# A feed-forward block on one core: the second stage as two nested levels of seven products

## What is computed

```python
def _L0_cond_ref(x, weight, bias, lora_a_weights, lora_b_weights, scaling_factors, adapter_id):
    base = jnp.einsum('bsi,oi->bso', x, weight) + bias
    a_sel = lora_a_weights[adapter_id]
    b_sel = lora_b_weights[adapter_id]
    scale = scaling_factors[adapter_id]
    low = jnp.einsum('bsi,bri->bsr', x, a_sel)
    delta = jnp.einsum('bsr,bor->bso', low, b_sel)
    return base + scale[:, None, None] * delta

def _L0_ffn_ref(x, codes, absmax, bias):
    w = _dequant_nf4(codes, absmax)
    out = jnp.einsum('bsd,od->bso', x, w)
    return out + bias

x = x + _L0_ffn_ref(_L0_cond_ref(x, ...), codes, absmax, bias)
```

## Time and profile before

| what | value |
|---|---|
| median of 3 runs | 2213.1 us (2212.15 to 2213.67) |
| span of the profiled execution | 2211.8 us, 1.3 us under the median of the runs |
| TensorE busy | 2166.8 us (98%) |
| VectorE busy | 1790.3 us (81%) |
| ScalarE busy | 1016.5 us (46%) |
| GpSimd busy | 46.8 us (2%) |
| DMA | 558.00 MB, mean 252 GB/s |
| granted TensorE clock | 0.994 of full |

### The profile page before, as it was taken

One profiled execution on the slowest core, in us unless ns is written; L12 is line 12 of the kernel. 1 busy time (PEld: TensorE's weight loads), 2 busy tenths in 40 slices (PEclk: granted clock), 3 DMA queues, 4 the chain that ended last, 5 costly groups with the idle time before them and its releaser, 6 DMA issues.

```text
span 2211.8 us, 31548 instructions
## 1 busy us (share of the span) xinstructions
PE 2166.8 (98%) x12104; PEld 1859.8 (84%) x12104; DVE 1790.3 (81%) x2647; ACT 1016.5 (46%) x1277; POOL 46.8 (2%) x55
## 2 busy tenths in 40 slices
PE   4899999999999999999999999999999999999999
PEld 4688788788878778899999988888988889888888
DVE  8899889768974664688778898888898887988887
ACT  8655555555553333444444443343443434443432
POOL 5100000000000000000000000000000000000000
PEclk8999999999999999999999999999999999999999
DMA  9688788887887897777777887777977877877775
GB/s 285 218 255 268 226 260 267 261 257 240 271 260 237 276 306 228 270 239 239 234 244 233 271 283 240 241 245 246 304 251 240 253 245 257 289 249 246 239 244 173
DMA packets 381172, 558.00 MB, mean 252 GB/s; under 512 B 23376, under 2 KB 234992, under 8 KB 380896
## 3 DMA queue, kind: packets, MB, share of 16 engines
q1 hardware_dynamic: 377712, 544.95, 77.6%
q0 software_dynamic: 3312, 11.03, 1.6%
HBM read 427.96 MB, written 128.99 MB: 252 GB/s over the span
## 4 chain that ended last, share of the span: by engine, by line
PE 91%; DVE 4%; DMA 3%; issue 1%; ACT 0%; SPq 0%; DVEq 0%; ACTq 0%
PE ps L1441 26%; PE ps L1273 14%; PE ps L1275 14%; PE ps L1274 14%; PE ps L1442 13%; PE ps L1445 4%; PE ps L1288 2%; PE ps L1444 2%; DMA rq<-xc_d 1%; PE ps L1321 1%; PE ps L1269 1%; DMA xc_d<-rq 1%; DMA xr<-xc_d 0%; DVE low_tw L966 0%; DVE tile L987 0%
## 5 line engine op out<-in xcount | busy, mean ns | idle before, releaser
L1441 PE MATMUL ps<-comb,xs 128*128 128x512 f32 x2527 | 903.3, 395 | 0.8 <-DVE comb L1047 0.8
L767 ACT CAST xs<-xr 128x1024 fp32r<-128x1024 f32 x427 | 448.3, 1051 | 629.8 <-DMA xr<-xc_d 628.9
L1442 PE MATMUL ps<-comb,xs 128*128 128x256 f32 x2527 | 707.8, 280 | 0.0
L1053 DVE TENSOR_TENSOR xs<-xr,xs 128x1024 fp32r<-128x1024 f32 x427 | 521.4, 1221 | 130.8 <-ACT xs L767 127.8
L1441 PEld LDWEIGHTS ps<-comb,xs 128*128 128x128 f32 x2527 | 474.3, 188 | 103.5 <-DVE comb L1047 1.1
L1442 PEld LDWEIGHTS ps<-comb,xs 128*128 128x128 f32 x2527 | 475.4, 188 | 14.5
L1273 PE MATMUL ps<-wq,tile 128*128 128x512 f32 x1088 | 468.2, 430 | 1.9 <-DVE tile L987 1.8
L1275 PE MATMUL ps<-wq,tile 128*128 128x512 f32 x1088 | 427.5, 393 | 0.0
L1274 PE MATMUL ps<-wq,tile 128*128 128x512 f32 x1088 | 426.1, 392 | 0.0
L1273 PEld LDWEIGHTS ps<-wq,tile 128*128 128x128 f32 x1088 | 205.2, 189 | 70.1 <-ACT cs L735 3.5
L1275 PEld LDWEIGHTS ps<-wq,tile 128*128 128x128 f32 x1088 | 204.9, 188 | 45.0
(11 more groups left out here) (119 smaller groups left out, 2219.8 us busy)
## 6 DMA issues: line engine op xcount, KB each, us to landing
xr<-xc_d SPq DMA_DIRECT2D x427, 512.0 KB, 4.0
raw<-in_L_cond_weight_dram SPq DMA_DIRECT2D x128, 512.0 KB, 4.8
xc_d<-rq SPq DMA_DIRECT2D x26, 1792.0 KB, 7.5
res<-in_x_dram SPq DMA_DIRECT2D x64, 512.0 KB, 5.2
out_dram<-res SPq DMA_DIRECT2D x128, 256.0 KB, 4.5
wc_d<-cs SPq DMA_DIRECT2D x32, 896.0 KB, 4.6
comb_raw<-wc_d SPq DMA_DIRECT2D x28, 1024.0 KB, 7.8
x_nat<-in_x_dram SPq DMA_DIRECT2D x104, 256.0 KB, 3.9
```

The source lines that it names most:

```text
L767: nc.scalar.copy(xs[f][:, HI, :, :], xr[f][:, LO, :, :]).then_inc(s_xhi, 1)
L1053: tt(xs[f][:, LO, :, :], xr[f][:, LO, :, :], xs[f][:, HI, :, :].bitcast(F32), ALU.subtract).then_inc(s_xlo, 1)
L1441: nc.tensor.matmul(bank[:, :], x_hi, both, start=(k == 0), stop=False)
L1442: nc.tensor.matmul(bank[:, 0:HW], x_lo, high, start=False, stop=False)
```

## The change

Stage 2 becomes two nested levels of seven products. The outer level is the seven combinations that stage 1 still makes (now with a 2 x 2 split of the full output, columns in halves of 1024 and inner dimension in halves of 1024); the inner level splits each outer product once more. The loop is over 56 units u = 8i + q: i is the outer combination (order `OUTER`), q the batch entry, and in each unit seven inner products k (order `INNER`) for two row tiles at once: 7 x 4 blocks x 3 matmuls with 512 output columns.

- **Inner weight sums**: SP loads four blocks of `wc_d` into `tb`, GpSimd makes four sums of 1024 elements (`sum_blocks`), SP stores them to `wi_d` and loads them from there as weights, in halves. This is done twice for each outer product.
- **Inner x sums**: SP loads two 512 KB blocks into `xg` once a unit, VectorE makes four sums of 512 elements (`sum_x`), then ScalarE and VectorE split seven tiles of 512 elements (`x_hi`, `x_lo`).
- **Adding up**: products 0, 2, 4, 6 accumulate in one PSUM bank or pair of banks, 1 and 3 in another; VectorE reads the running value after each product and adds it to `r_sb` (in the first and last eight units ScalarE copies four of the seven). TensorE waits for the reading of product k before it starts product k + 2 (`evacuated`). The sums of outer products go to `m_d` in DRAM and come back as a base (`load_base`, `load_total`); output rows are stored from unit 32 on.
- In units 0 to 31 the 512 columns are cut in two matmuls of 256, the second with 16 columns of lora A in four products of seven. From unit 32 on they are one matmul of 512.
- The residual is an identity matrix added to the combined weight in stage 1 (16 matmuls of 128 columns).
- In the last eight units (u from 48 on) two totals are finished: GpSimd and VectorE each add 2048 elements (`add_last`).
- The jobs of the last strip of stage 1 also load blocks, make inner sums and split the first weights.

Core of the diff (stage 2 of each engine; loads of the last strip of stage 1, lora and constants left out):

```diff
 # SP
+            for u in range(NU):
+                i, q = divmod(u, QB)
+                turn = q == QB - 1 and i < LAST
+                if 1 <= u <= BOTH:
+                    store_sums(u - 1, 1)
+                if u > BOTH:
+                    for m in range(2):
+                        store_total(u - 1, m)
+                if u + 1 < NU:
+                    sp.wait_ge(s_xlo, NF * (u + 1))
+                    load_x(u + 1)
+                if u + 1 < LOWS:
+                    load_a(u + 1)
...
+                for k in range(NF):
+                    if turn:
+                        sp.wait_ge(s_prod, NF * u + k + 1)
+                        for c in range(2):
+                            load_half_comb(i + 1, INNER[k], c)
+                    if k == 1 and QB <= u + 1 < BOTH:
+                        load_base(u + 1)
...
+                    if k == 1 and u >= BOTH:
+                        for m in range(2):
+                            load_total(u, m)
+                    if k == 3 and i < LAST:
+                        if q == 1:
...
+                            load_blocks(i + 1, 0)
+                        if q == 3:
+                            for n in range(4):
+                                store_sum(i + 1, 0, n)
+                            load_blocks(i + 1, 1)
+                        if q == 5:
+                            for n in range(4):
+                                store_sum(i + 1, 1, n)
+                if u < BOTH:
+                    store_sums(u, 0)
 # GpSimd
+            def sum_blocks(i, c):
...
+                tt(b11, b12, b11, ALU.subtract).then_inc(s_ws, 1)
+                pool.wait_ge(s_wl[B22], arrived[B22])
+                tt(b12, b22, b12, ALU.subtract).then_inc(s_ws, 1)
+                pool.wait_ge(s_ws, 4 * n + 1)
+                tt(b22, b22, b11, ALU.subtract).then_inc(s_ws, 1)
...
+                tt(b21, b21, b22, ALU.subtract).then_inc(s_ws, 1)
+            def add_last(u):
...
+                pool.wait_ge(s_lev, 4 * (u - BOTH + 1))
+                tt(total[1][:, :, :, :], total[1][:, :, :, :], r_sb[u % 2][:, :, :, :], ALU.add).then_inc(s_fin[1], 1)
+            for u in range(NU):
+                i, q = divmod(u, QB)
+                if i < LAST and q in (2, 4):
+                    sum_blocks(i + 1, q // 2 - 1)
+                if u >= BOTH:
+                    add_last(u)
 # VectorE
+    LO_STEPS = {2: [0], 3: [1], 4: [2, 3], 5: [4], 6: [5, 6], 7: [7], 8: [8, 9], 9: [10], 10: [11, 12], 11: [13]}
+            for u in range(NU):
+                i, q = divmod(u, QB)
+                for k in range(NF):
...
+                    if not fresh(u) or k not in COPIED:
+                        add_product(u, k)
...
+                    if u >= BOTH and k == 5:
+                        add_lora_pair(u, 0)
+                        add_lora_pair(u, 1)
+                    if u >= BOTH and k == 6:
+                        add_last(u)
+                        add_lora_pair(u, 2)
+                        add_lora_pair(u, 3)
...
+                    if k == 1 and u + 1 < LOWS:
+                        a_difference(u + 1)
...
+                    if u + 1 < NU and k in (2, 3, 4):
+                        sum_x(u + 1, {2: (0, 1), 3: (2,), 4: (3,)}[k])
+                    if u + 1 < NU:
+                        for f in {3: (A11, SS1), 4: (S2,), 5: (S4, S3), 6: (A12, A22)}.get(k, ()):
+                            x_lo(u + 1, f)
+                    for n, h in lo_halves(u, k):
+                        comb_lo(n, h)
 # TensorE
+            def multiply(u, k):
...
+                if k in (2, 3, 4, 6):
+                    evacuated(u, {2: 0, 3: 1, 4: 2, 6: 4}[k])
...
+                for kt in range(QT):
...
+                    if not split:
+                        ins = three(big[:, bank, :], x_hi, x_lo, w_hi[:, 0:SW], w_lo[:, 0:SW], first, last and not lora,
+                                    not opens)
+                        continue
+                    for n, (x, w) in enumerate(((x_hi, w_hi), (x_hi, w_lo), (x_lo, w_hi))):
+                        begin, end = first and n == 0, last and n == 2
+                        nc.tensor.matmul(big[:, bank, 0:HW], x, w[:, 0:HW], start=begin, stop=end,
+                                         skip_group_check=not opens)
+                        ins = nc.tensor.matmul(big[:, bank + 1, 0:wide], x, w[:, HW:HW + wide], start=begin, stop=end,
+                                               skip_group_check=not opens)
-            for i in range(PRODUCTS):
...
-                for k in range(0 if is_wide(i) else HK):
-                    last = three(psum, xs[f][:, HI, k, :], xs[f][:, LO, k, :], cw[f][:, k, HI, cols],
-                                 cw[f][:, k, LO, cols], k == 0, k == HK - 1)
```

More of the change, by code:

```diff
@@ L82, in adaln_ffn_kernel @@
     NF = 7
-    WITH_LOW = {A11: 0, A12: 1, S2: 1, S3: 2}
     GROUP_OF = [S3, A22, A11, A12]
@@ L196, in wide_before, with fresh, adds_of, added @@
-    def wide_before(i):
-        return sum(is_wide(n) for n in range(i))
+    def fresh(u):
+        return u < QB or u >= BOTH
+    def adds_of(u):
+        return 3 if fresh(u) else 8 if u >= LOWS else 7
+    def added(u, k):
+        before = sum(adds_of(n) for n in range(u))
+        if fresh(u):
+            return before + k - 2
+        return before + k + 1 + (1 if u >= LOWS and k > 4 else 0)
+    def copied(u, k):
+        return 4 * (u if u < QB else QB + u - BOTH) + COPIED.index(k) + 1
@@ new lines, in halves_of, with half_at, half_bytes @@
+    def halves_of(i):
+        if i:
+            return [(f, c) for f in INNER for c in range(2)]
+        return [(A11, 0), (A11, 1), (SS1, 0), (SS1, 1), (S2, 0), (S4, 0), (S2, 1), (S4, 1),
+                (S3, 0), (S3, 1), (A12, 0), (A12, 1), (A22, 0), (A22, 1)]
+    def half_at(i, f, c):
+        return 2 * NF * i + halves_of(i).index((f, c)) + 1
+    def half_bytes(i, f, c):
+        if f not in DIRECT:
+            return 16 * (i + 1)
+        return 32 * (i + 1) + (16 if (f, c) == (S4, 1) else 0)
@@ L253, in adaln_ffn_kernel @@
-        low_rep = [at(f"low_rep{i}", 195 + 0.5 * i, [P, P], F32) for i in range(2)]
+            wide = CW if f in WITH_LOW else SW
+            cw.append(at(f"comb{f}", cw_kb[f], [P, QT, 2, wide], F32R))
+            cr.append(at(f"comb_raw{f}", cw_kb[f], [P, QT, 2, wide], F32))
+        xs_kb = {A11: 184, SS1: 188, S2: 192, S4: 105, S3: 109, A12: 113, A22: 117}
+        xs = [at(f"xs{f}", xs_kb[f], [P, 2, QT, P], F32R) for f in range(NF)]
+        xr = [at(f"xr{f}", xs_kb[f], [P, 2, QT, P], F32) for f in range(NF)]
@@ new lines, in adaln_ffn_kernel @@
+        xg = at("xg", 176, [P, 2, 2, QT, P], F32)
+        tb = [at(f"tb{i}", 160 + 4 * i, [P, HALF, SW], F32) for i in range(4)]
+        total = [at(f"total{i}", 160 + 8 * i, [P, 2, 2, SW], F32) for i in range(2)]
+        r_sb = [at(f"r_sb{i}", kb, [P, 2, 2, SW], F32) for i, kb in enumerate((97, 49))]
+        a_b = at("a_b", 59, [P, 2, 3, QT, R], F32R)
+        a_br = at("a_br", 59, [P, 2, 3, QT, R], F32)
+        g_b = at("g_b", 57, [P, 2, SW], F32R)
+        g_raw = at("g_raw", 196, [P, 2, SW], F32)
@@ L623, in _ @@
+            for m in range(2):
+                store_total(NU - 1, m)
+            for n in range(2):
+                sp.wait_ge(s_rst[n], 32 * (BOTH // 2))
+                sp.wait_ge(s_out[n], 32 * QB)
         @block.gpsimd
@@ new lines, in add_product @@
+            def add_product(u, k):
+                t, n = [(0, 0), (1, 1), (0, 1), (0, 1), (1, 1), (0, 0), (1, 0)][k]
+                bank = Y_BANK if k in (1, 3) else z_bank(u) if k == 5 else x_bank(u)
+                dve.wait_ge(s_prod, NF * u + k + 1)
+                if fresh(u):
+                    dve.wait_ge(s_cpy, copied(u, 2))
+                elif k >= 3 and k < 6:
+                    dve.wait_ge(s_add, added(u, {3: 2, 4: 1, 5: 0}[k]))
+                else:
+                    dve.wait_ge(s_rld[u % 2], 32 * ((u - QB) // 2 + 1))
+                dst = quarter_of(r_sb[u % 2], t, n)
+                tt(dst, main(bank, u, k not in (1, 3)), dst, ALU.add).then_inc(s_add, 1)
@@ L1158, in _, with add_last @@
+            def add_last(u):
+                dve.wait_ge(s_add, added(u, 5))
+                dve.wait_ge(s_cpy, copied(u, 6))
+                dve.wait_ge(s_lev, 4 * (u - BOTH) + 2)
+                tt(total[0][:, :, :, :], total[0][:, :, :, :], r_sb[u % 2][:, :, :, :], ALU.add).then_inc(s_fin[0], 1)
             for b, value in zip(bends, BENDS):
```

1043 lines of the change are left out of this document (607 added, 436 removed).

## The result

| | before | after |
|---|---|---|
| median of 3 runs | 2213.1 us | 2256.4 us (2254.7 to 2259.3) |
| ratio | | 1.0198, 95% interval 1.0182 to 1.0214 |
| span of the profiled execution | 2211.8 us | 2254.6 us |
| granted TensorE clock, mean | 0.994 | 0.957 |

What follows compares the result with a forecast made beforehand. The prediction took TensorE to bound the kernel: last product at 2039.8 us without new stalls, plus 56 (turns), 31 (GpSimd), 12 (change of stage), 36 (last outer product) and 16 (end) makes 2190.8, forecast 2192 us. Range 2122 to 2255.

Steps and rivals of the forecast that it cites:

- Plain units: Stage 2 units without turns or GpSimd sums: 20.0 us, from unit 32 on 19.0 and lora; VectorE's work costed at nothing.
- rival C: Stage 2's 40 middle units: each of five waits on adds leaves a 0.25 us gap, 50 us, 2242 us; chance 0.07.
- GpSimd's sums: Inner weight sums in stage 2 hold VectorE up: 3.1 us for each of ten groups, 31 us.
- Six turns: Changes of outer product: VectorE needs 37.9 us where TensorE's ten products take 28.6; 9.3 us each, 56 us.
- rival B: Turns and last outer product: x and lora A come late, adds stand behind; 30 + 22 us, 2244 us; chance 0.25.
- The last outer product: Units from 49 on: next x load waits behind the stores of both totals; 6 us for 6 units, 36 us.
- Stage 1 to 2: Change of stage: the third product waits 7.7 us for its weights, four further products about 1 us each; 12 us.
- Rival D: Stalls in stage 2: each of twelve is followed by one product at 1.2 GHz, 32 us, 2224 us; chance 0.07.
- The end: After the last product: copy, two instructions, GpSimd and two stores of 512 KB, 16 us where it was 4.2.
- Rival A: Stage 2: the covers hold, turns cost 26 us, GpSimd nothing, last eight units half; 2113 us; chance 0.13.

Runs made afterwards that it cites:

- e2: Kernel after with GpSimd's inner weight sums of outer products 1 to 6 made on 8 of 256 columns; 2224.4 us.
- e5: Kernel after with the inner weight sums of outer products 1 to 6 made by VectorE instead of GpSimd; 2222.7 us.
- e9: e5 plus x load ahead of GpSimd's total, turn's x and lora A loads ahead of weights and stores, then last total on VectorE; 2160.0 us.
- e3: Kernel after with weight loads of 32 of 256 columns at the turns to outer products 1 to 5; 2222.0 us.
- e12: e11 plus earlier low parts of x in unit 0, and block loads behind the base load with their sums in units 3 and 5; 2148.4 us.
- e10: e2 with GpSimd's inner weight sums of outer product 0 also made on 8 of 256 columns; 2218.0 us.
- e11: e9 with the next unit's lora A load issued first in SP's list of every unit; 2149.2 us.

## Why the prediction was wrong, point by point

- **Plain units**: right, 19.9 to 20.5 us where 20.0 and 19.0 with lora were given (from unit 32 on matmuls of 512 columns start every 0.232 us and not every 0.227; the 1% that was added covers it), and rival C (a gap at each wait) is out: no gap in any of them.
- **GpSimd's sums**: mechanism right, and the sum too, 33 us by e2 for 31, but that is in part luck: units 1 and 4 of the first outer product, costed at nothing, took 26.1 and 22.3 us (19.9 in e2), while units 36 and 44 took nothing over plain; and the slow matmuls behind these stalls are in the 33 us and were not in the term. The rows showed in one instruction what e2, e5 and e9 showed in sum. The Trainium skill (SBUF — State Buffer, SBUF: two separate sides) has GpSimd and VectorE take turns at shared ports for a whole instruction; the trace agrees, 5.14 us for two of 0.68 beside GpSimd, and 0.68 for the one from PSUM.
- **Six turns**: the first of the two steps that failed. The 9.3 us were VectorE's shortage with all data in time, and e3 (8.1) and e12 (10.3 over plain) bear it out: in turn 8 of e12 A lands 4.7 us and x 5.4 us before VectorE takes it. But I took loads as in time and left late ones to rival B. Both come: 13.4 a turn, 24 us more than predicted. B's mechanism (A and x late, VectorE before them with adds behind) is in the rows, though it is VectorE's last low part of x that sends them out, and the weights in the queue that slow them; its price of 5 us a turn is what small loads gave (5.5). It was wrong to make a rival of something that adds to the forecast.
- **The last outer product**: 51 for 36 us. The chain was right, the x load behind the total. I left out that VectorE's low parts of x stand beside GpSimd's 4.9 us, though I had priced that very effect two paragraphs before, and the clock, about 2.2 us a unit by the distances between matmuls.
- **Stage 1 to 2**: 31 for 12 us, the poorest term. I had counted the chain of weights alone, not the wait for A and x, which the rows below (of the kernel after) show at the start and again in unit 0. In unit 0 TensorE stands 15.6 us, 7.8 of them before one add of VectorE, 4.3 before a low part of weights and 3.6 before a copy of ScalarE, and with the clock at 0.74 it is busy 9.0 us longer than in a plain unit. e10 moved unit 0 by 3 us, e11, with A first, by 4. What stands behind the rest of the waits no run tells; it stays open.

```profile
904.69 0.23 DVE L1334 TENSOR_TENSOR a_br<-a_br 128x64 f32<-128x64 f32 x1 [17.68 <-DMA a_br<-a_sel_d]
...
939.91 0.23 DVE L1334 TENSOR_TENSOR a_br<-a_br 128x64 f32<-128x64 f32 x1 [5.63 <-DMA a_br<-a_sel_d]
```

- **The clock**: the second step that failed. The sum had no clock in it. Its terms for waits add up to 135 us (12, 56, 31, 36), and TensorE stood 125.4 us in stage 2 and 6.9 before it, 132; but it was busy 1206.0 us where plain units take 1132. Of these 74 us the distances between the starts of matmuls give 64 to the clock: 8 in unit 0, 27 in the turns, 13 in the thirteen units, 13 in units 49 to 54, some 2 elsewhere. That is twice D's 32, since D counted twelve stalls and at a turn there are several, and e12 still has a half of it (busy 1166.5). Rival D was right as an addition too. How much a full clock would have saved no run shows: where TensorE waits for VectorE it would then only have waited longer. The Trainium skill (TensorE: Matmul & The Clock Gate, HAM oscillation) says that waits between groups of matmuls make the clock fall again and again; the trace agrees, 0.50 for 6.0 us after the stall of 3.6.
- **The end**: right, 15.5 for 16.
- **Rival A** is out: the covers did not hold.

The range failed because B (+52) and D (+32) were each set against the forecast with small chances, while by their mechanisms both belonged on top of it: 2192 and a part of each is what was measured.

## What to carry to other kernels

When a change takes away the lead of the bounding engine, add up late transfers, engine hold-ups and clock falls instead of choosing among them: here one stall held several of them. In an in-order list, a small late load (here the 64 KB of lora A) must not stand before work whose data is there; issue it first. Look also at what releases a load: here the x load waited for a low part of an engine that was late itself. Before giving GpSimd sums in SBUF beside a VectorE that works from SBUF, price VectorE's standing time: here the "fuller" engine did the same work in half the time (1.22 us a sum for 2.4 to 2.9) and the whole got 34 us faster by it.
